# A fused transformer step on one core: expert products in quarter slots, layer-norm scaling and odd experts moved off VectorE

## The reference, cut to what matters

```python
x = x + cross_attention(_layernorm(x), ctx)          # 16 heads of 16, softmax over 1601 keys, then Wo
x = x + moe(_layernorm(x))                           # 8 experts 256x256, top 1
x = x + window_attention(ctx, _layernorm(x))         # tanh([context, q] @ W_c.T), a window of 256 keys
x = x + slot_mixer(_layernorm(x))                    # gelu router, top 8 of 64 slots, GRU, slot attention

# moe
probs = softmax(x @ router_w.T + router_b)
y_all = einsum('bsd,eod->bseo', x, expert_w) + expert_b
out = y_all[top1] * max(probs)
```

## Time and profile before

| | us |
|---|---|
| time, median of 3 runs | 1205.0 (1202.1 to 1208.08) |
| profiled execution, its own time | 1201.54 |
| its span, first to last instruction | 1199.9 |
| TensorE busy | 1021.9 (85%) |
| VectorE busy | 809.4 (67%) |
| ScalarE busy | 562.3 (47%) |
| GpSimd busy | 44.1 (4%) |
| mean granted TensorE clock | 0.916 of full |

### The profile page before, as it was taken

The page is one execution under the profiler, slowest core; times in us unless marked ns, Lnnn a source line. Parts: engine busy times, 40 slices in busy tenths (PEclk is TensorE's granted clock), DMA queues, the critical chain, the costliest instruction groups (busy, mean ns, idle before and its releaser), DMA issues.

```text
span 1199.9 us, 13638 instructions
## 1 busy us (share of the span) xinstructions
PE 1021.9 (85%) x4812; PEld 411.0 (34%) x4812; DVE 809.4 (67%) x1820; ACT 562.3 (47%) x1019; POOL 44.1 (4%) x54
## 2 busy tenths in 40 slices
PE   6446999999988998988899989888999898696656
PEld 3322233232333333433433334333333343243424
DVE  4446978787767777777677777776777677644232
ACT  4121066667644545666445556664455466301210
POOL 3110000000000000000000000000000000100000
PEclk9876599999989999999899999998999899978665
DMA  8996000000100000001000000010000000100512
GB/s 248 146 112 220 1 1 14 15 1 14 33 1 14 1 14 1 14 1 49 1 14 1 14 1 14 1 49 1 14 1 14 1 15 1 49 0 1 146 49 70
DMA packets 44238, 40.65 MB, mean 34 GB/s; under 512 B 10109, under 2 KB 42334, under 8 KB 43914
## 3 DMA queue, kind: packets, MB, share of 16 engines
q1 hardware_dynamic: 41594, 38.17, 13.6%
q10 hardware_dynamic: 2496, 1.35, 0.8%
q0 software_dynamic: 80, 0.26, 0.2%
HBM read 29.52 MB, written 10.59 MB: 33 GB/s over the span
## 4 chain that ended last, share of the span: by engine, by line
issue 46%; PE 26%; DVE 11%; DMA 6%; SPq 5%; ACT 2%; DVEq 2%; POOL 2%; POOLq 0%; ACTq 0%
DVE mx L1125 8%; PE ps_o L814 7%; PE ps_e L977 7%; PE ps_m L735 6%; DMA k_parts<-alphaT 2%; SPq L395 2%; DMA k_stack<-q_stack 2%; DMA xres<-in_x 1%; SPq L443 1%; PE ps_m L1040 1%; ACT probs L616 1%; PE ps_m L926 1%; SPq L419 1%; PE ps_m L929 1%; DMA x<-xres 1%
## 5 line engine op out<-in xcount | busy, mean ns | idle before, releaser
L1125 DVE TENSOR_REDUCE mx<-ps_m 128x1 f32<-128x401 f32 x1102 | 578.0, 568 | 203.7 <-PE ps_m L735 196.2
L616 ACT ACTIVATE probs<-ps_e 128x512 f32<-128x512 f32 (+1 forms) x832 | 472.6, 597 | 405.6 <-PE ps_e L977 404.8
L735 PE MATMUL ps_m<-k_stack,q_stack 99*128 99x401 bf16 x1102 | 356.7, 353 | 40.8 <-DVE mx L1125 40.0
L977 PE MATMUL ps_e<-q_stack,k_stack 101*128 101x512 bf16 (+1 forms) x832 | 326.2, 392 | 8.3 <-ACT probs L616 6.2
L814 PE MATMUL ps_o<-probs,v_heads 128*32 128x512 f32 (+1 forms) x1664 | 226.9, 618 | 0.0
L977 PEld LDWEIGHTS ps_e<-q_stack,k_stack 101*128 101x128 bf16 (+1 forms) x832 | 82.6, 99 | 302.1 <-ACT probs L616 207.5
L735 PEld LDWEIGHTS ps_m<-k_stack,q_stack 99*128 99x128 bf16 x1102 | 109.9, 100 | 175.9 <-DVE mx L1125 124.8
L880 PE MATMUL ps_m<-expert_w,xnT 128*128 128x512 f32 x256 | 130.8, 612 | 16.2 <-DVE xb L1254 16.2
L1254 DVE SCALAR_TENSOR_TENSOR xb<-ps_m,hot,xb 128x256 f32<-128x256 f32 x112 | 54.1, 483 | 18.3 <-PE ps_m L880 9.2
L880 PEld LDWEIGHTS ps_m<-expert_w,xnT 128*128 128x128 f32 x256 | 47.7, 196 | 48.3 <-DVE xb L1254 24.7
L814 PEld LDWEIGHTS ps_o<-probs,v_heads 128*32 128x32 f32 (+1 forms) x1664 | 33.0, 108 | 64.7 <-issue 56.1
(11 more groups left out here) (215 smaller groups left out, 617.3 us busy)
## 6 DMA issues: line engine op xcount, KB each, us to landing
q_stack<-q_parts SPq DMA_DIRECT2D x114, 64.0 KB, 2.2
k_stack<-k_parts SPq DMA_DIRECT2D x18, 256.0 KB, 14.0
q_parts<-attn_chunk SPq DMA_DIRECT2D x6, 384.0 KB, 5.8
expert_w<-in_expert_wT SPq DMA_DIRECT2D x2, 1024.0 KB, 6.0
xres<-in_x SPq DMA_DIRECT2D x4, 512.0 KB, 3.8
x<-xres SPq DMA_DIRECT2D x4, 512.0 KB, 3.2
probs<-x SPq DMA_DIRECT2D x1, 2048.0 KB, 9.7
out<-probs SPq DMA_DIRECT2D x4, 512.0 KB, 2.9
```

The source lines that it names most:

```text
L616: act.activation(probs[0:n, k % 2, h, :], ps_e[h % 2][0:n, :], ACT.Exp).then_inc(s["exp_done"], 1)
L735: pe.matmul(ps_m[:, (UNITS * n1 + u) % RING, 0:SPLIT], qst[0:MAX_ROW, g, h, P * t:P * t + P], kst[0:MAX_ROW, HG * g + h, QUARTER_START[q]: ...
L977: pe.matmul(ps_e[h % 2][0:n, :], kst[0:ROWS, HG * g + h, P * st:P * st + n], qst[0:ROWS, g, h, :], start=True, stop=True).then_inc(s["qk_r ...
L1125: dve.tensor_reduce(mx[:, q, col:col + 1], ps_m[:, (UNITS * n1 + u) % RING, 0:SPLIT], AX.X, ALU.max)\
```

## The change

- Expert products: two matmuls of 512 columns two quarters apart become four of 256 columns, one a quarter. The y and score products also put one matmul into each quarter (they had two).
- Scaling in the layer norms: ScalarE computes `rstd * x + off`. GpSimd computes `off = -mean * rstd` with three more small operations (`shift`).
- Experts: VectorE still does the even expert of each pair. ScalarE multiplies the odd one by its gate, into `xres` for j = 0 and into a slice of `work2` for j = 1 to 3, and frees the bank. It waits for VectorE's even part first. GpSimd adds the three slices to `xres`. After j = 3 VectorE adds `xres` to `xb` and takes that tile's bn_stats.
- gateT and the bias jobs move from behind e3 and e15 to behind e1 and e2.
- The due quarters become: y0 14, y1 18, t1a 34, router 39, e0 43, e1 49, gateT 53, e2 55, gb0 61, gb1 63, e3 65, then every four up to e10 93, e11 99, e12 103, e13 107, e14 113, e15 117, t2a 132, score0 137, score1 141, aTa 154, z0 159, z1 168, t3a 189, h 194, logits 200, slots 212, alphaT 218. What lies past 208 is no longer finished at the end of the loop but runs on in the first quarters of the loop after it.

```diff
+JOBS = [("ota", None, 9, 3), ("otb", "ota", 2, 3), ("y0", "otb", 3, 6), ("y1", "y0", 4, 6), ("t1a", "y1", 16, 3),
+        ("t1b", "t1a", 2, 3), ("router", "t1b", 3, 2), ("e0", "router", 4, 6), ("e1", "e0", 4, 6), ("gateT", "e1", 4, 3),
+        ("e2", "gateT", 1, 6), ("gb0", "e2", 4, 4), ("gb1", "gb0", 2, 4), ("e3", "gb1", 2, 6)]
+JOBS += [(f"e{i}", f"e{i - 1}", 4, 6) for i in range(4, NE)]
+JOBS += [("t2a", f"e{NE - 1}", 15, 3), ("t2b", "t2a", 2, 3),
+         ("score0", "t2b", 3, 6), ("score1", "score0", 4, 6), ("aTa", "score1", 13, 3), ("aTb", "aTa", 2, 3),
+         ("z0", "aTb", 3, 9), ("z1", "z0", 8, 9), ("t3a", "z1", 21, 3), ("t3b", "t3a", 2, 3), ("h", "t3b", 3, 5),
+         ("logits", "h", 6, 2), ("slots", "logits", 12, 6), ("alphaT", "slots", 4, 3)]
...
+            def shift():
+
+                pool.tensor_tensor(mean_2[:], mv[:, :, 0], neg_half[:], ALU.mult)
+                pool.drain()
+                pool.tensor_tensor(mean_2[:], mean_2[:], rstd[:], ALU.mult)
+                pool.drain()
+                pool.tensor_tensor(off[:], mean_2[:], mean_2[:], ALU.add).then_inc(s["off_ready"], 1)
...
                 for i in range(1, 4):
                     rsqrt(NC + 3 * c + i)
+                    shift()
+                    if i == 1:
+                        for t in range(TT):
+                            for j in range(1, 4):
+                                pool.drain()
+                                pool.wait_ge(s["odd_scaled"], NE * c + 4 * t + j + 1)
+                                pool.tensor_tensor(xres[:, t, :], xres[:, t, :], work2[:, j, :], ALU.add)\
+                                    .then_inc(s["odd_added"], 1)
...
+            def normal(src, at, n):
+
+                for t in range(TT):
+                    yield at + t // 2
+                    if t == 0:
+                        act.wait_ge(s["off_ready"], n)
+                    last = act.activation(xn[:, t, 0:D], src[:, t, :], ACT.Identity, bias=off[:, t:t + 1],
+                                          scale=rstd[:, t:t + 1])
+                last.then_inc(s["xn_ready"], 1)
...
+                for i in range(NE):
+                    t, j, name = i // 4, i % 4, f"e{i}"
+                    yield AT[name] + 5
+                    act.wait_ge(s["even_added"], NE * c + i + 1)
+                    if j:
+                        need(act, s["odd_added"], 3 * (TT * c + t) + j - 3)
+                    dst = work2[:, j, :] if j else xres[:, t, :]
+                    last = act.activation(dst, bank(name, c)[:, D:2 * D], ACT.Identity, scale=hot8[:, t, 2 * j + 1:2 * j + 2])
+                    taken(last, name, c)
+                    act.drain().then_inc(s["odd_scaled"], 1)
...
                     name, t, j = f"e{i}", i // 4, i % 4
                     yield AT[name]
                     bank_free(pe, name, c)
-                    for k in range(KT):
-                        yield AT[name] + 2 * k
-                        mm = pe.matmul(bank(name, c), xnT[:, k, P * t:P * t + P], expert_w[:, k, CT * j:CT * j + CT],
-                                       start=(k == 0), stop=(k == KT - 1))
+                    for n in range(2):
+                        for k in range(KT):
+                            yield AT[name] + KT * n + k
+                            mm = pe.matmul(bank(name, c)[:, D * n:D * n + D], xnT[:, k, P * t:P * t + P],
+                                           expert_w[:, k, CT * j + D * n:CT * j + D * n + D],
+                                           start=(k == 0), stop=(k == KT - 1))
                     filled(mm, name, c)
...
+                    yield AT[f"e{i}"] + 4
+                    dve.drain()
+                    wait_filled(dve, f"e{i}", c)
+                    dve.scalar_tensor_tensor(out=xb[:, t, :], in0=bank(f"e{i}", c)[:, 0:D], scalar=hot8[:, t, 2 * j:2 * j + 1],
+                                             in1=(xb if j else xa)[:, t, :], op0=ALU.mult, op1=ALU.add)\
+                       .then_inc(s["even_added"], 1)
...
+                    if j == 3:
+                        yield AT[f"e{i}"] + 7
+                        dve.wait_ge(s["odd_added"], 3 * (TT * c + t + 1))
+                        dve.tensor_tensor(xb[:, t, :], xb[:, t, :], xres[:, t, :], ALU.add)
+                        dve.drain()
+                        dve.bn_stats(bst[:, t, :], xb[:, t, :])
...
-            def chunk(c):
-                work = begin(behind(c - 1)) if c else None
+            def chunk(c, work):
+                old, work = work, begin(behind(c - 1)) if c else None
...
+                        go_on(old, HG * (SLOTS + k) + h)
                         go_on(work, HG * k + h)
-                go_on(work, NEVER - 1)
-
+                return work
```

More of the change, by code:

```diff
@@ L129, in job_numbers @@
         for q in range(HG * SLOTS):
+            if c >= 2:
+                order += [(name, c - 2) for name in AT if AT[name] == HG * SLOTS + q]
             if c:
@@ L1258, in behind @@
+                    if j == 3:
[4 more added lines that the diff above has]
+                        dve.bn_stats(bst[:, t, :], xb[:, t, :])
                 dve.drain()
+                for t in range(TT):
+                    last = dve.bn_aggr(mv[:, t, :], bst[:, t, :])
+                last.then_inc(s["var_ready"], 1)
```

118 lines of the change are left out of this document (56 added, 62 removed).

## The result

| | before | after |
|---|---|---|
| median of six runs | 1205.6 us (1202.1 to 1208.2) | 1217.5 us (1212.6 to 1220.0) |
| profiled execution, its span | 1201.54, 1199.9 | 1216.7, 1215.0 |
| TensorE / VectorE / ScalarE / GpSimd busy | 1021.9 / 809.4 / 562.3 / 44.1 us | 1031.8 / 772.2 / 618.2 / 85.9 us |

The ratio is 1.0094, 95% interval 1.0067 to 1.0122: the changed kernel is 0.9% slower. 1198 was predicted, with a range to 1214. In what follows all stretches are from the two profiled executions, whose spans differ by 15.2 us (1215.0 - 1199.9, from unrounded ends 15.16).

A forecast was written before the change was run, and what follows sets the result against it. It took TensorE to bound the expert phase, with VectorE holding it up around norms and at banks. Loops -21, boundaries and leftover +5, last chunk +8.9 gave -7 us: 1198 us predicted, range 1186 to 1214.

The forecast's parts named there:

- loops without their ends: Three loops with background work: products, bank waits, norms and clock together, -21 us.
- two crossings: Slots and alphaT running into the next chunk at two boundaries: two bank waits at each, +3.5 us (0 to +6).
- leftover behind the last loop: Bare work after the last loop, from ScalarE's exponentials to the slots product: +1.5 us (0 to +5).
- last chunk alone: Last chunk's uncovered work: norms, expert products, bias products and new waits lengthen it by 8.9 us (+4 to +13).
- Work across the chunk's end: Late slots and alphaT steps at two boundaries and behind the last loop: +3.5 and +1.5, +5 us together.
- Odd halves: Expert products in the loops: ScalarE frees the bank earlier than VectorE did, shortening bank waits, -8 us (0 to -15).
- Normalisations: Norms in the loops: four scalings move to ScalarE, half their time showing; -7.5 us (+3 to -15).
- Split products: Expert products as 256-column matmuls: +0.04 us an expert, +2 us in the loops (0 to +5), +1.2 in the last chunk.
- Clock: Half-clock stretches in the three loops: shorter TensorE stands save some, -5.5 us (0 to -9); the weakest term.
- GpSimd: Odd-expert additions: about 0.74 us each, hidden in the loops; the shared-interface rule could add 0.4 us for each of 16.
- Rival 2: Loops: odd halves hold ScalarE's in-order queue, delaying exponentials, and norm scalings cost in full (+3); 1218 us, chance 0.20.
- Rival 1: Whole kernel: changes mostly cancel, half-clock stretches stay or bank waits shrink half as much; 1203 to 1208 us, chance 0.30.

The follow-up runs named there:

- e4_spill_early: Changed kernel with three lags shortened by 1 or 2 quarters, work still running on past the chunk's end: 1195.5 us, ratio 0.9929.
- e1_drain: Changed kernel with each loop finishing its background work at its own end, due quarters as in the change: 1209.3 us, ratio 1.0037.
- e2_early: Changed kernel with each loop finishing its work at its own end and three lags 1 or 2 quarters shorter: 1194.9 us, ratio 0.9921.
- p3_odd: Kernel before with only the odd expert halves scaled on ScalarE and summed by GpSimd: 1187.9 us, ratio 0.9896.
- p2_actnorm: Kernel before with only the three norms scaled on ScalarE and their shift computed on GpSimd: 1213.6 us, ratio 1.0092.
- e8_norm1: e7_odd_quarters with the first norm of chunks 0 to 2 also scaled on ScalarE with GpSimd's shift: 1180.8 us, ratio 0.9792.
- e7_odd_quarters: Kernel before with quarter products, and odd halves on ScalarE and GpSimd in chunks 0 to 2 only: 1185.9 us, ratio 0.9833.
- p1_quarters: Kernel before with only the expert products split into four matmuls of 256 columns, one a quarter: 1199.7 us, ratio 0.9961.
- e5_tail: e2_early with the last chunk's norms, expert products, sums and bias products done as in the kernel before: 1186.8 us, ratio 0.9853.

## Why the prediction was wrong

The sign of the loops' own terms was right; the price of the late steps at the chunk's end was not. Predicted and measured, in us:

| step | predicted (bounds) | measured |
|---|---|---|
| loops without their ends | -21 | -15.8 |
| two crossings | +3.5 (0 to +6) | +14.1 |
| leftover behind the last loop | +1.5 (0 to +5) | +5.2 |
| last chunk alone | +8.9 (+4 to +13) | +10.5 |
| start | 0 | +1.2 |
| sum | -7 | +15.2 |

**Work across the chunk's end: the step that failed.** It makes 10.6 + 3.7 = 14.3 of the 22 us by which the sum was off; at its predicted price the measured sum would be +0.9, level with the kernel before. The two waits were named rightly: the first transpose waits 2.15 us for the slots' bank, and the second 0.99 us for the bank that ScalarE empties at 11. That is the first transpose's bank, which the second has to share because alphaT has the other one in between. A third stand, 0.91 us before y0, was not named. Three things were left out. The price was taken from the mean bank wait of the expert phase (1.27 us), but in quarter 9 VectorE comes to the slots' bank behind two steps of the attention and two maxima. The alpha chain had been spread over quarters that now lie beside the loop's first ones, and TensorE waits for it too (0.81 us). And the cost was counted as standing alone: half clock for 6.8 us came with it, and against e4_spill_early TensorE is busy 3.3 us longer a crossing. For the leftover I took ScalarE's exponentials to the slots product as hidden for the most part; TensorE stood 3.75 us behind them, and the slots product took 3.69 us, most of it at half clock. e4_spill_early shows the step most directly: with slots and alphaT four and six quarters earlier, still crossing, the crossings and the leftover give 14.6 us back. e1_drain shows that finishing at the end in place of crossing gives little (2.2 to 2.3 us an end in the profile) while the steps stay late. The other part of the 22 us that e2_early and e4_spill_early win lies in the expert phase, so the late steps don't carry the whole difference.

**Odd halves (-8, bounds 0 to -15).** Right in mechanism, too small: p3_odd's loops are 19.4 us shorter, past the bound. 11.6 us are the bank waits (15.2 to 3.6), where the prediction let a wait keep half of its length; 6.9 us are less busy time, put down to the clock, which it kept apart as a term of its own (-5.5) and so had the sum of the two at -13.5. In the changed kernel itself the bank waits fell by 7.1 us (15.2 to 8.1), near the 8. Its expert phase takes 89.6 us over chunk 0's in the three loops; before it was 95.2 (quarters 38 to 118), in p3_odd 78.0 and in e4_spill_early 77.9. So two thirds of what the odd halves are worth were lost by where the change put the experts and by the stretch at half clock.

**Normalisations (-7.5, bounds +3 to -15).** Wrong at the due quarters of before: +5.4 (p2_actnorm), past the bound. The step priced four scalings and let half of them show. It left out that ScalarE, called to the norm at a fixed quarter, waits for a GpSimd chain that has become three operations longer, with exponentials behind it. In the changed kernel the longer lags repair this: from six quarters before a norm's first transposes to five behind them, the nine norms of the loops take 24.8 us over chunk 0's, against 33.5 before, 41.6 in p2_actnorm and 31.5 in e4_spill_early, whose lags are shorter. Not all of the 8.7 us need be the norm's, as the other steps lie otherwise too. The price is then paid at the chunk's end, where the lags pushed slots and alphaT. So the two terms that I had summed as independent are one trade. e8_norm1 shows that the first norm gains without any lag: its quarters 20 to 38 take 5.9, 7.1 and 5.9 us over chunk 0's, against 8.8, 8.9 and 8.8 in e7_odd_quarters.

**Split products (+2 in the loops, +1.2 in the last chunk).** -0.4 and -0.4 in p1_quarters's profile, and in its timed runs 3.8 us less than before: no cost; where a gain of 3.8 us would sit, the profile does not show, so that is left open. The -2 for the y and score products was not measured by itself.

**Clock (-5.5, the weakest term).** Three loops at 0.99, 0.96 and 0.98 in place of 0.98, 0.99 and 0.97: nothing was gained. One stretch of 10.2 us at half clock in chunk 2's expert phase (from 624.7) and one of 6.8 at each crossing took the place of those that went. In e8_norm1, at the due quarters of before, it is 1.00, 0.99 and 1.00.

**The last chunk (+8.9).** Right within its bounds. From the parts: norms +6.1 for three (4.95 predicted; in the changed kernel the first one takes 1.54 us longer from its statistics to its transposes, 1.65 predicted), odd halves +3.3 (2.2 predicted), quarters -0.4 (+1.2 predicted). The waits at e2 and at j = 3 are there (0.98 us once and 0.5 us three times in the trace, 0.7 and 0.5 predicted). Why the parts' 9.0 us became 10.5 stays open. e5_tail confirms it from the other side, 9.2 us back.

**GpSimd.** 0.728 us an addition, 0.74 predicted; hidden in the loops. The Trainium skill (GPSIMD Engine Reference, 1. Specifications) has GpSimd and VectorE share SBUF interfaces where VectorE reads two SBUF inputs. 48 maxima ran while an addition did, at 566 ns on average, the 1054 others at 568; these read PSUM, so the rule's case is not in them. VectorE's sum of xb and xres waits for the additions and never ran beside one for more than 0.03 us (16 sums, 418 ns). So the up to 0.4 us a sum did not come. But the trace agrees with the rule in a place outside the loops, where both VectorE's difference and GpSimd's operation read two SBUF inputs:

```profile
27.06 3.01 POOL L546 TENSOR_TENSOR expert_w<-q_stack 16x1601 f32<-16x1601 f32 x1 [16.89 <-ACT q_stack L626]
29.13 1.49 DVE L1105 TENSOR_TENSOR work<-work,alphaT 128x512 f32<-128x512 f32 x1 [2.37 <-ACT alphaT L609]
31.88 0.68 DVE L1105 TENSOR_TENSOR work<-work,alphaT 128x512 f32<-128x512 f32 x1
```

Alone the difference takes 0.68 us; beside GpSimd's operation it ends 0.55 us after that one's end, at 30.62. In e4_spill_early, where it starts earlier in GpSimd's operation, it takes 2.46 us and ends 0.54 us after it, and in the kernel before 1.11 and 0.55. It is held until GpSimd is done.

**Rivals.** Rival 2 had the time right (1218) for a wrong reason: the odd halves don't hold the scores up (no such wait in quarters 43 to 122), and the norms, whose full price it had as +3, take less in the changed kernel than before. That its time came true is luck: the loss is in the crossings, the leftover and the last chunk, of which no rival priced the first two higher. Rival 1 was right that the short stretches at half clock stay, and its times, 1203 to 1208, were 10 us and more too low for the same reason as the forecast's.

## What to carry to other kernels

When background work is laid out in due quarters, a longer lag at one step is paid where the last steps land: work out the last steps' quarters and write down, for each, which bank, which queue and which cover they meet there. A step that falls past the covered stretch costs its full chain, and the granted clock after its stands on top; here that was 19 us against 16 us gained inside the loops. Before an engine that works in order is given a wait, look at what queues behind it and at what the move spares the other engine: ScalarE's stand of 1.5 us at the first norm was worth it, that of 2.7 us at the second was not. And keep a second way, without the hand-overs, for the stretch that nothing covers: e5_tail won 9 us by it.

## What was not expected of the hardware

- At each crossing of the changed kernel the granted clock fell to half behind four stands of 2.1 us in all, and stayed there for 6.8 us: pairs of the slots product took 1.12 us in place of 0.65, and a crossing with the same matmuls 20.2 us of busy time in place of 16.9. Stands of 2.4 us in e4_spill_early and the one of 2.15 us here were followed by no fall.
- A VectorE operation with two SBUF inputs that starts while GpSimd works on two SBUF inputs is held until GpSimd ends: 1.11 to 2.46 us in place of 0.68, by how early it came.
- Four scalings with bias and scale columns on ScalarE take 2.07 us for 128x256 in the last chunk (590 to 596 ns one by itself), against 1.38 on VectorE; 2.1 was estimated.
- Splitting 512-column products into 256-column ones, with twice the weight loads, cost nothing that the profile can show (888.3 against 888.6 us in the loops, 165.1 against 165.5 behind them).
